# A decoder layer on one core: the work at the change of batches put in another order

## The reference

```python
x = layernorm(x + attn(x))          # 32 heads, 8 key/value groups, rope, causal, and a second,
                                    # "latent" attention with its own keys and values
x = layernorm(x + fake_quant(x) @ fake_quant(ctx))     # ctx: 2 x 1024 x 1024
x = layernorm(x + fp8_sim(x) @ fp8_sim(weight))        # scaled by the maximum of |x| and of |weight|
# attn(x) = softmax(q k') v @ w_o + softmax(q lk') lv @ w_lo,
# lq = x @ w_lq, lk = lq @ w_lk, lv = x @ w_lv
```

## Time and profile before

| what | value |
|---|---|
| median of 3 runs | 2533.32 us (2532.18 to 2535.01) |
| the profiled execution's own time | 2531.58 us |
| its span | 2529.6 us |
| busy: PE, DVE, ACT, POOL | 98%, 69%, 45%, 36% of the span |
| chain of work that ended last | PE 94%, DVE 3%, issue 1%, ACT 1% |
| one chunk on PE at full clock (12 matmuls, 1239.32 to 1242.04 us) | 2.72 us |
| lq on PE | 1208.55 to 1219.72 us |
| DVE idle before batch 1's first rotation | 2.63 us, until 1226.60 us |
| batch 1's first q rotation starts | 1267.31 us |
| rounding of a ctx piece (line 856): median, longest of 32 | 0.486, 2.448 us |

### The profile page before, as it was taken

One profiled execution on the slowest core, in us unless ns is written; L12 is line 12 of the kernel. 1 busy time (PEld: TensorE's weight loads), 2 busy tenths in 40 slices (PEclk: granted clock), 3 DMA queues, 4 the chain that ended last, 5 costly groups with the idle time before them and its releaser, 6 DMA issues.

```text
span 2529.6 us, 40729 instructions
## 1 busy us (share of the span) xinstructions
PE 2468.4 (98%) x12456; PEld 2088.7 (83%) x12456; DVE 1734.9 (69%) x3589; ACT 1131.9 (45%) x2576; POOL 921.8 (36%) x696
## 2 busy tenths in 40 slices
PE   7899999999999999999989999999999999999998
PEld 6688888888888888887767888888888888888877
DVE  5676767767676767665587676767767677667656
ACT  3444434344444535444365453544444354544551
POOL 4334242433434242432543424243342524334210
PEclk9999999999999999999999999999999999999999
DMA  5323231312223232322423323222232323234411
GB/s 179 89 80 92 64 104 58 98 56 75 87 75 95 62 98 60 90 64 87 136 89 131 105 70 109 69 85 77 83 104 71 109 70 106 60 90 147 154 34 67
DMA packets 124407, 226.26 MB, mean 89 GB/s; under 512 B 13088, under 2 KB 21408, under 8 KB 124192
## 3 DMA queue, kind: packets, MB, share of 16 engines
q1 hardware_dynamic: 119552, 216.91, 28.2%
q10 hardware_dynamic: 4768, 8.39, 0.9%
HBM read 206.37 MB, written 18.87 MB: 89 GB/s over the span
## 4 chain that ended last, share of the span: by engine, by line
PE 94%; DVE 3%; issue 1%; ACT 1%; DMA 0%; POOL 0%; SPq 0%; PEldq 0%; ACTq 0%; DVEq 0%
PE bank_a L1200 16%; PE bank_a L1202 16%; PE bank_a L1201 16%; PE bank_b L1200 13%; PE bank_b L1201 13%; PE bank_b L1202 13%; PE bank_b L1248 5%; PE bank_b L1517 1%; PE bank_a L1325 0%; DMA probs<-xt 0%; DVE probs L809 0%; PE bank_b L1384 0%; PE bank_b L1500 0%; POOL w_lo L414 0%; DVE acc L845 0%
## 5 line engine op out<-in xcount | busy, mean ns | idle before, releaser
L414 POOL TENSOR_TENSOR w_lo<-w_raw,w_hi 128x512 fp32r<-128x512 f32 x632 | 844.0, 1344 | 1419.2 <-ACT w_hi L478 1411.2
L478 ACT ACTIVATE w_hi<-w_raw 128x512 fp32r<-128x512 f32 x632 | 392.9, 626 | 287.9 <-DMA w_raw<-wstream 141.5
L1200 PE MATMUL bank_a<-w_hi,o_hi 128*128 128x512 f32 x1024 | 410.7, 401 | 9.0 <-DVE acc L845 4.8
L1202 PE MATMUL bank_a<-w_hi,o_lo 128*128 128x512 f32 x1024 | 403.5, 394 | 0.0
L1201 PE MATMUL bank_a<-w_lo,o_hi 128*128 128x512 f32 x1024 | 403.1, 394 | 0.0
L826 DVE TENSOR_TENSOR pT_lo<-bank_b,pT_hi 128x512 fp32r<-128x512 f32 (+1 forms) x384 | 207.0, 594 | 267.1 <-ACT pT_hi L521 267.1
L515 ACT ACTIVATE probs<-probs,row_min 128x512 f32<-128x512 f32 (+3 forms) x512 | 281.6, 552 | 240.8 <-DVE row_min L809 238.4
L525 ACT ACTIVATE o_hi<-bank_b 128x512 fp32r<-128x512 f32 x128 | 76.8, 600 | 455.4 <-PE bank_b L1202 455.4
L820 DVE TENSOR_SCALAR probs<-probs,row_inv 128x512 f32<-128x512 f32 (+3 forms) x512 | 261.4, 570 | 4.5
L1200 PEld LDWEIGHTS bank_a<-w_hi,o_hi 128*128 128x128 f32 x1024 | 193.5, 189 | 44.3 <-issue 7.8
L1200 PE MATMUL bank_a<-xT_hi,w_hi 128*128 128x512 f32 x544 | 214.2, 394 | 14.4 <-POOL w_lo L414 14.4
(11 more groups left out here) (176 smaller groups left out, 4785.4 us busy)
## 6 DMA issues: line engine op xcount, KB each, us to landing
w_raw<-wstream SPq DMA_DIRECT2D x632, 256.0 KB, 2.7
stage<-ctx SPq DMA_DIRECT2D x32, 256.0 KB, 2.7
stage_w<-wf SPq DMA_DIRECT2D x32, 256.0 KB, 2.8
q_scratch<-stage_q SPq DMA_DIRECT2D x32, 128.0 KB, 2.3
wf_hi_scratch<-piece_hi SPq DMA_DIRECT2D x16, 256.0 KB, 3.0
wf_lo_scratch<-stage_w SPq DMA_DIRECT2D x16, 256.0 KB, 3.3
wf_hi<-wf_hi_scratch SPq DMA_DIRECT2D x8, 512.0 KB, 7.9
wf_lo<-wf_lo_scratch SPq DMA_DIRECT2D x8, 512.0 KB, 11.8
```

The lines of the kernel that those rows point to most:

```text
L414: nc.gpsimd.tensor_tensor(w_lo[:, s], w_raw[:, r], w_hi[:, s].bitcast(F32), ALU.subtract).then_inc(lo_done, 1)
L478: nc.scalar.activation(w_hi[:, s], w_raw[:, r], ACT.Copy).then_inc(hi_done, 1)
L1200: nc.tensor.matmul(dst, still[0], move[0], start=start, stop=False)
L1202: return nc.tensor.matmul(dst, still[1], move[0], start=False, stop=stop)
```

## The change

DVE adds the first half before it splits the new x, and splits two quarters between the two additions; the moments of x1 follow at once. The square roots on ACT move from the eleventh chunk of batch 1's first group to a place ahead of lq_hi. Two of the four normalisations of x1 go ahead of the first rotation, two stay in the group. POOL's maximum over the partitions moves from behind the tail into batch 1's first group, after the `low` of chunk 6, and its scale on DVE into that group. The second piece of ctx is quantised after the masks of unit 1 instead of ahead of `lv_lo`; that line is shared by all groups.

```diff
--- before.py
+++ after.py
@@ -436,6 +436,10 @@
                 G = g + KVH * b
                 for c in range(CHUNKS):
                     low(b, g, c, c)
+                    if c == 6 and first and b:
+
+                        pool.wait_ge(w_run_done, 2 * KVH)
+                        nc.gpsimd.partition_all_reduce(col(W_ALL), col(W_RUN), P, RMAX).then_inc(w_all, 1)
                     if c == 12 and first:
                         wait(pool, colsum_ready, 2 * b)
                         nc.gpsimd.memset(col_part[:], 0.0).then_inc(cols_added, 1)
@@ -454,10 +458,6 @@
                     group(b, g, False)
                 for c in range(C_TAIL):
                     low(b, KVH, c, TAIL_POS + c)
-                if b == 0:
-
-                    pool.wait_ge(w_run_done, 2 * KVH)
-                    nc.gpsimd.partition_all_reduce(col(W_ALL), col(W_RUN), P, RMAX).then_inc(w_all, 1)
 
             for t in range(TT):
                 add_corr(TT + t, corr1)
@@ -608,9 +608,6 @@
 
                 if c == 3:
                     load_q2_0()
-                if c == 11:
-                    for t in range(TT):
-                        root_of_x1(0, t)
                 if c in (12, 13):
                     shift_x1(c - 12)
                 if c in (14, 15):
@@ -683,6 +680,9 @@
                         high(0, 0, quarter - C_LQ, LQ_POS + quarter, (0, chunk(0, 0, quarter - C_LQ)))
                 for c in range(C_LQ):
                     high(b, 0, c, c, (0, chunk(b, 0, c)))
+                if b:
+                    for t in range(TT):
+                        root_of_x1(b - 1, t)
                 for l in range(2):
                     act.wait_ge(*((chunk_used, chunk(b, 0, 0)) if l else (lq_ready, b + 1)))
                     nc.scalar.activation(lq_hi[:, l], BANK_A[l][:], ACT.Copy).then_inc(lq_hi_done, 1)
@@ -944,19 +944,19 @@
                                                 v_hi[:].bitcast(F32).rearrange("p t n -> p (t n)"),
                                                 ALU.subtract).then_inc(v_lo_done, 1)
                         quantise_piece(b, G, 0)
+                        if first and b:
+                            dve.wait_ge(w_all, 1)
+                            fp8_scale(WS, col(W_ALL))
                         weight_piece(b, g, 0)
                     if i == HG and first and b:
-                        for t in range(TT):
-                            moments_of_x1(b - 1, t)
-                        for t in range(TT):
-                            layernorm_of_x1(b - 1, t)
+                        layernorm_of_x1(b - 1, 2)
+                        layernorm_of_x1(b - 1, 3)
                         round_x1(0)
                         round_x1(1)
                     if i == HG + 1 and first and b:
                         round_x1(2)
                         round_x1(3)
                 rotated_low(G, ROPES - 1, *tiles[-1][2:])
-                quantise_piece(b, G, 1)
                 for t in range(TT):
                     dve.wait_ge(lv_hi_done, TT * G + t + 1)
                     nc.vector.tensor_tensor(lv_lo[:, t], BANK_B[t][:], lv_hi[:, t].bitcast(F32),
@@ -964,6 +964,7 @@
                 mask_scores(G, 0)
                 normalise(G, 0)
                 mask_scores(G, 1)
+                quantise_piece(b, G, 1)
                 for u in range(UNITS):
                     if u < 2 and first and b:
                         for t in range(TT):
@@ -1047,23 +1048,26 @@
                     link(nc.vector.memset(ones[:], 1.0))
                     nc.vector.tensor_copy(ident_b[:], ident_sb[:]).then_inc(tables, 1)
                 if b:
-                    dve.wait_ge(w_all, 1)
-                    fp8_scale(WS, col(W_ALL))
                     correct(0, 0)
                     correct(0, 1)
+                    layernorm_of_x1(0, 0)
+                    layernorm_of_x1(0, 1)
                 group(b, 0, True)
                 with dve.Fori(1, KVH) as g:
                     group(b, g, False)
                 o_low(KVH * (b + 1) - 1, UNITS - 1)
                 if b + 1 < B:
                     p = 4 * KVH * (b + 1) - 2
-                    for half in range(2):
-                        x_low(b + 1, 2 * half)
-                        x_low(b + 1, 2 * half + 1)
-                        add_part(b, p + half, half, chunk(b, KVH, 4 * half + 4), False)
-                        if half == 0:
-                            for t in range(TT):
-                                half_stats_of_x1(b, t, 0)
+                    add_part(b, p, 0, chunk(b, KVH, 4), False)
+                    x_low(b + 1, 0)
+                    x_low(b + 1, 1)
+                    for t in range(TT):
+                        half_stats_of_x1(b, t, 0)
+                    x_low(b + 1, 2)
+                    x_low(b + 1, 3)
+                    add_part(b, p + 1, 1, chunk(b, KVH, 8), False)
+                    for t in range(TT):
+                        moments_of_x1(b, t)
 
             def moments_of(i, n):
                 for half in range(2):
```

## The result

The changed kernel takes 2525.95 us (median of 6 runs, 2522.69 to 2528.77), the kernel before 2532.75 in runs between them (6 runs, 2530.84 to 2535.01). The ratio is 0.997, with a 95% interval of 0.996 to 0.9981: faster by 6.8 us, inside the range of 2518.0 to 2527.5, at 4.2 us above the single figure of 2521.8 and just above the 2519 to 2525 that the forecast's own mechanism was given. The profiled execution of the changed kernel took 2527.03 us, with a span of 2525.0. One execution of a later kernel, e3, took 4129.71 us at a mean granted clock of 0.556 and stands in no median, range or comparison here.

A forecast was written before the change was run, and what follows sets the result against it. The prediction took the kernel to be bound by PE (98% busy). Its terms summed to 9.6 - 1.9 + 3.8 = 11.5 us, so 2533.32 - 11.5 = 2521.8 us, with 8 in 10 in 2518 to 2527.5.

The forecast's parts named there:

- the forecast's own mechanism: The main forecast for the whole change, 2521.8 us, given 62% and its own range of 2519 to 2525.
- The last rotations: Batch 1's first group: with three pieces left there, q rotations start at about 1261.5 instead of 1267.3.
- the signs: Trace checks: no acc wait and clock 1.00 at the batch change, lq 9.6 us earlier, 1 to 3 us w_lo wait.
- the three terms: Change of batches 9.6 us gained, maximum in the group 1.9 lost, first scores of batch 1 3.8 gained.
- the first scores: First scores of batch 1: first values start 3.8 us earlier; bounds 1.0 to 5.5.
- The boundary: Change of batches: additions first and the maximum moved away let lq start at 1198.95 for 1208.55, 9.6 us gained.
- The maximum: Batch 1's first group: the reduction delays low(7), so PE loses 1.9 us at chunk 7; bounds 0 to 3.5.
- The same 14.7 us: POOL's reduction with idle 6.87 before and 6.75 after, expected again behind low(6) of batch 1's first group.
- (1): Rival: POOL's way back after the maximum is free, no loss at chunk 7, 13.4 us gained, 2519.9; 12%.
- (2): Rival: corrections and ctx piece collide with DVE, first values start no earlier, 7.7 us gained, 2525.6; 13%.
- (3): Rival: late moments make the roots ahead of lq_hi late beyond their cover, 3.5 us gained, 2529.8; 7%.
- (4): Rival: the ctx piece ahead of pT_lo in the 15 other groups loses 18 us, 2539.8; 6%.

The follow-up runs named there:

- e3: The changed kernel with POOL's maximum moved into the tail, behind the low of the fourth tail chunk; 2521.98 us.
- e1: The changed kernel with POOL's maximum put back in its old place behind the tail; 2530.06 us.
- e4: The changed kernel with the second additions ahead of the last quarter of x; 2524.02 us.
- e8: The kernel before with additions first, the last quarter of x behind them and the maximum in the tail; x1's part and ctx piece unmoved; 2521.75 us.
- e5: The changed kernel with the maximum inside the tail and the second additions ahead of the last quarter of x; 2516.93 us.
- e6: The kernel before with only the second ctx piece moved behind the masks of unit 1, in all groups; 2534.29 us.
- e2: The kernel before with only the maximum, and its scale, moved to chunk 6 of batch 1's first group; 2533.89 us.
- e7: The changed kernel with the second ctx piece put back ahead of lv_lo; 2526.69 us.

## Why the prediction was right, and what was off in it

**Right: where the time comes from, and each sign.** The wait for acc at the fifth tail chunk and that for lv_lo are gone, the maximum gives way ahead of lq and takes its price at chunk 7, the later groups keep PE full. The two ends of the change were forecast as needing each other ("without this move the reordered additions would gain nothing"), and e1 shows it. The last rotations came about where forecast too: the q rotations begin 20.4 us after chunk 7 (less the 2.9 us of lower clock), for 19.5 forecast (1261.5 - 1242.04) and 25.3 before. Of the signs, clock 1.00 held for the tail chunks (1187.1 to 1197.9 us) and not for lq (0.87), and lq's first product came 8.1 us earlier after the anchor, not 9.6. But the three terms were not equally good; counted from the anchor the sum is 6.6 - 6.0 + 3.7 = 4.3 us, where 9.6 - 1.9 + 3.8 = 11.5 was forecast. Two of the three lie outside the bounds that they were given (7.0 to 9.8, and a loss of 0 to 3.5). Set against the medians (6.8) the fault is smaller, 4.7 us. That the time fell inside the range is in part luck: the range left room for the first scores to fail, they didn't, and the room was used up by the two terms that were bounded too narrowly.

**The boundary: 9.6 forecast, 6.6 measured.** The failed step is "lq's first bank is free at 1198.9, and PE waits some 0.6 us where it could have begun at 1198.3". Beside a busy POOL two of the four quarters of x took 1.80 and 2.06 us instead of 1.23, each of which the next load or addition waits for, and the wait came to 2.25 us. The trace of the kernel before had shown as much: one of its quarters took 1.93 us while POOL ran from 1187.31 to 1192.54. e1 has the counterpart: with the maximum behind the tail POOL idles from 1192.25 to 1198.90, and the last quarter takes 1.23. The two rows, the kernel before first, then e1:

```profile
1189.47 1.93 DVE L991 TENSOR_TENSOR xT_lo<-probs,xT_hi 128x1024 fp32r<-128x1024 f32 x1 [1.50 <-ACT xT_hi L504]
```

```profile
1196.35 1.23 DVE L992 TENSOR_TENSOR xT_lo<-probs,xT_hi 128x1024 fp32r<-128x1024 f32 x1 [1.74 <-ACT xT_hi L504]
```

So the move of the maximum, which lets POOL split the lq chunks early, is itself what makes the last quarter slow. By the Trainium skill, SBUF — State Buffer, section on the two separate sides, a VectorE operation with two inputs in SBUF, as this one is, waits out a whole GpSimd operation that reads SBUF and has begun first. These rows fit that; I had used the section for the ctx piece, and not here.

The late lq start is 1.5 of the 3.0 us missing. The other 1.5 us are the lower clock in lq, of which the sum had nothing: it treated a short wait as costing its own length, as in the earlier trace rows, where 3.04 us idle were followed by full clock. e4 confirms the rest of the term: with the order repaired it gives 10.6.

**The maximum: 1.9 forecast, about 6 measured.** The place and the mechanism were right, the size was not. "The same 14.7 us" were 15.9: the pause on the way back took 8.58 us in place of 6.75, the reduction itself 0.38 in place of 1.09. So chunk 7 waited 2.96 us, still inside the bound of 3.5. The larger part of the miss is the 2.9 us of lower clock behind that wait, which no term and no bound had. The price on POOL differs by place: 14.2 to 14.7 us in the tail and behind it (e8, e1, e5, e3, before; 15.2 in e6), 15.7 to 16.2 in the group (e2, e7, the changed kernel, e4). Why the way back is longer in the group stays open; no run here tests it.

**The first scores: 3.8 forecast, 3.7 measured** (from chunk 7 on: 136.17 - 67.80 = 68.37 before, 131.92 - 64.34 = 67.58 after, so 0.8 net, and 2.9 for the clock). e5 against e8 gives 3.9 without the disturbance. The steps hold one for one: q1T copies bound the first cross product (two waits of 0.53), the exponentials waited 2.31 us for POOL's corrections and began 51.4 us after chunk 7, again less the 2.9 (forecast 1293.1 - 1242.04 = 51.1; before 56.0), the moved ctx piece took 0.9 us behind the mask (forecast 1.0). As expected of e6, moving that piece alone gives nothing, and by e7 it doesn't pay with the corrections made earlier either.

**The rivals.** (1), a free way back, is excluded by every trace with the maximum in it: 6.75 to 9.35 us. The Trainium skill, GPSIMD Engine Reference, section 2.1 Instruction dispatch, speaks of the first call to a freshly loaded kernel alone, with about 6 us; whether the operation behind the reduction is such a call again it doesn't say. The idle time ahead of the reduction is 6.43 to 7.54 us in the ten traces, a little more than that. (2), no gain at the first scores, would have given 2525.6, close to the 2525.95 measured: the total alone would have confirmed the wrong story. The anchored distances and e5 against e8 rule it out. (3) fell: the roots ended at 1210.3, with 1.9 us of idle time left on ACT before lq_hi (cover of 2.1 forecast). (4) fell with the full later groups, and with e6.

**The spread.** The two kernels that meet short waits at lq and at chunk 7 in one execution (the changed one, e7) spread over 6.1 us (6 executions) and 7.4 (10); e4, e5 and e8 over 1.3 to 1.5 (5 each), e3 over 2.2, and the kernel before over 4.2 in 6. That fits a clock that falls in some executions and not in others, as the two traces of lq show, but it was not traced run by run.

## What to carry to other kernels

Work that has one long price on an otherwise idle engine (here 14 to 16 us of POOL for one tiny reduction) has to be put where that engine's idle time and the lead of its next result over the bounding engine cover the price together, as 12.95 us and the 3.0 us by which the next low was early did for 14.4. The place is found from the idle times in that engine's own timeline: the same reduction held up lq behind the tail, cost 6 us of PE's time in the group, and nothing inside the tail. In a hand-written queue, order by who is waited for first: one operation ahead of the additions, 1.2 us by itself and 2.06 beside POOL, cost PE 4 us. And cost a new wait on the bounding engine at more than its length, since lower clock may follow; check a total that fits against distances from an anchor, as a total can lie in its range (2525.95 here) though two of its three terms are outside theirs.

## What the runs showed of the hardware that I had not expected

Whether PE's clock falls after a short wait is not told by the length of the wait alone. Ahead of lq 3.04 us were followed by full clock in the kernel before, 3.49 in e6 and 2.14 in e7, but 2.23 (e3) and 2.25 (the changed kernel) by 1.2 GHz for some 3 us. In the kernel before and e6 PE had already run at 1.2 GHz for some 5 us after the stall for acc, until 8.6 us before this wait; whether that has to do with it no run tests. At chunk 7 the wait of 2.96 us in the changed kernel was followed by 1.2 GHz for 6 us, 2.76 (e2) and 3.30 (e4) for some 3, and in e7 2.78 us by 0.8 us at full clock and only then by 1.2 GHz, for 3.4 us. The price of the reduction on POOL is almost all before and after it (0.38 us of its own in most traces, 0.45 in e6, 1.09 in the kernel before), and it comes in each place where it was put.
